# Final blocks in two turns of 128 nodes on one PSUM bank, and a second bank of feature sums for the dense blocks of a graph layer

## The reference

```python
src_h = h[src] @ W_msg.T + b_msg
emb = edge_embed[jnp.clip(edge_type, 0, NUM_EDGE_TYPES)]
messages = jax.ops.segment_sum(src_h + emb, dst, num_segments=num_nodes)
gi = messages @ W_ih.T + b_ih
gh = h @ W_hh.T + b_hh
r = jax.nn.sigmoid(i_r + h_r)
z = jax.nn.sigmoid(i_z + h_z)
n = jnp.tanh(i_n + r * h_n)
h_new = (1.0 - z) * n + z * h
out = layernorm(x + h_new)
```

## Time and profile before

| | before |
|---|---|
| median of 3 runs | 1285.8 us |
| lowest, highest run | 1283.81, 1469.57 us |
| the profiled execution's own time | 1292.56 us |
| its span | 1290.4 us |
| PE busy (matmuls) | 1011.8 us, 78% |
| DVE busy | 846.6 us, 66% |
| ACT busy | 626.9 us, 49% |
| POOL busy | 758.1 us, 59% |
| granted TensorE clock, mean | 0.924 of full speed |

### The profile page before, as it was taken

How to read it: one execution, slowest core, us unless ns; L and a number is a source line. 1 busy time by engine, 2 the same in 40 slices (tenths; PEclk the granted TensorE clock), 3 DMA queues, 4 the chain that set the end, 5 groups by cost and what they waited for, 6 DMA issues and landing times.

```text
span 1290.4 us, 23001 instructions
## 1 busy us (share of the span) xinstructions
PE 1011.8 (78%) x8241; PEld 634.0 (49%) x8241; DVE 846.6 (66%) x2672; ACT 626.9 (49%) x1215; POOL 758.1 (59%) x807
## 2 busy tenths in 40 slices
PE   5535587888888887878888787888888787988794
PEld 1114354555545454555555554555555555555462
DVE  7503557667776676766777667767677677667644
ACT  4342314355545464545655556545565465555523
POOL 7725546565665666566656666656666666566640
PEclk9666588898999999999999999999999999999998
DMA  7629212222323223322323323323333332233331
GB/s 232 177 65 334 74 34 61 75 74 77 78 77 90 73 79 80 90 75 79 90 78 80 87 78 85 82 74 90 79 88 84 84 90 77 79 86 89 84 87 31
DMA packets 95665, 116.97 MB, mean 91 GB/s; under 512 B 20027, under 2 KB 81271, under 8 KB 95544
## 3 DMA queue, kind: packets, MB, share of 16 engines
q0 software_dynamic: 36608, 75.94, 22.1%
...
## 4 chain that ended last, share of the span: by engine, by line
PE 51%; DVE 18%; issue 13%; another core or an unknown queue 9%; ACT 6%; DMA 1%; SPq 1%; DVEq 0%; ACTq 0%
PE psf L1097 20%; PE psb L1082 12%; DVE ohk L862 4%; PE pAB L1026 4%; DVE ohl L868 4%; PE psg L1065 3%; PE pAB L1040 3%; DVE ohk L865 2%; PE psg L1061 2%; ACT mem L1213 2%; PE psg L1069 2%; DVE ohs L844 2%; PE pAB L1043 1%; DMA arena<-in_x 1%
## 5 line engine op out<-in xcount | busy, mean ns | idle before, releaser
L604 POOL DMA_INDIRECT xg<-x_split,idx x676 | 640.8, 948 | 405.4 <-remote 161.1
L1097 PE MATMUL psf<-mem 128*128 128x384 bf16 x2548 | 585.2, 334 | 11.5 <-issue 6.2
L1213 ACT CAST mem<-psb 128x432 f16<-128x432 f32 x832 | 392.9, 524 | 412.0 <-PE psb L1082 286.4
L1082 PE MATMUL psb<-ohk,ohl 128*128 128x108 bf16 (+3 forms) x1801 | 401.1, 263 | 143.4 <-issue 89.5
L862 DVE TENSOR_TENSOR ohk<-table_bank,prm 128x392 bf16<-128x392 f16 (+3 forms) x421 | 260.6, 619 | 113.3 <-PE psb L1082 70.7
L1082 PEld LDWEIGHTS psb<-ohk,ohl 128*128 128x128 bf16 x1801 | 167.7, 100 | 315.8 <-issue 163.7
L1097 PEld LDWEIGHTS psf<-mem 128*128 128x128 f16 x2548 | 223.6, 100 | 108.1 <-issue 30.7
L891 DVE TENSOR_TENSOR mem<-mem,psg 128x120 f32 (+10 forms) x191 | 56.7, 297 | 210.5 <-remote 159.2
L868 DVE TENSOR_TENSOR ohl<-table_bank,prm 128x512 bf16<-128x512 f16 x421 | 174.3, 414 | 0.0
L604 POOL DMA_INDIRECT xg<-in_x,idx x88 | 84.2, 957 | 76.0 <-PE psg L1069 39.7
L865 DVE TENSOR_TENSOR ohk<-table_bank,sort 128x40 bf16<-128x40 f16 (+3 forms) x421 | 102.5, 244 | 0.0
...
## 6 DMA issues: line engine op xcount, KB each, us to landing
...
```

The lines of the kernel that those rows point to most:

```text
L604: pool.indirect_dma_start(out=xg[:, p % RING, :] if split else xg32(p % RING), out_offset=None, in_=x_d if split else x, in_offset=bass.In ...
L1082: ins = pe.matmul(psb[:, bank % NB, held * HC:(held + m) * HC], ohl[:, e % KB, :], ohk[:, e % KB, d * HC:(d + m) * HC], start=(k == 0), st ...
L1097: pe.matmul(psf[:, 0:3 * H], Bb[q % 2][0:kk, HT + h, :], xs[0:kk, h, :, :].rearrange("p c f -> p (c f)"), start=(h == 0), stop=(h == HI - ...
L1213: act.copy(Bb[q % 2][:, :, n:n + MOST], psb[:, bank % NB, 0:MOST * HC].rearrange("p (d h) -> p h d", h=HC)).then_inc(S["s_eb"], 1)
```

## The change

The final blocks but for two get the gates in two turns on one bank: `hh0`, `su0`, `rz0`, `t20` for the first 128 nodes, then `hh1`, `su1`, `rz1`, `t21` for the others. `hh1` waits on PE until `t20` is done (`s_t2` counts halves now). A block then has 13 slots, of which four go with a group (five at the end). The bank that comes free is a second bank of `psf`: the dense blocks use the two in turn, so F pieces wait for the C of the block before last only. S, T and C get the places 0.06, 0.14, 0.19, the F pieces are spread evenly from 0.045 on, and those that pass 1 go over into the next block. DVE's writing of the one-hot matrices of four slots stands behind the slot whose completion it waits for, where that is later than its old place.

```diff
@@ -50,17 +50,18 @@
 FIRST = 4
-STEPS = (3, 4)
+STEPS = (4, 5)
 READY = 10
-SHIFT = 5
+SHIFT = 8
+WIDE_SHIFT = 5
 TURN_AT = (15, 18)
...
 BW = HC * FB // 2
-SETTLED = (0.02, 0.06, 0.10)
-CLEAR = 0.17
+SHIFTED = 0.045
+SETTLED = (0.06, 0.14, 0.19)
 
@@ -164,21 +165,27 @@
 
-STAGES = ("cn", "hh", "su", "rz", "t2", "th", "yt", "bn", "sd", "ln")
-SLOTS = (("cn",), ("hh",), ("su", "rz"), ("t2", "th", "zero"), ("yt",), (), ("bn",), ("sd",), ("ln",))
+STAGES = ("cn", "hh0", "su0", "rz0", "t20", "hh1", "su1", "rz1", "t21", "th", "yt", "bn", "sd", "ln")
+SLOTS = (("cn",), ("hh0",), ("su0", "rz0"), ("t20",), ("hh1",), ("su1", "rz1"), ("t21", "th", "zero"), ("yt",), (), ("bn",),
+         ("sd",), ("ln",))
+WIDE = ("hh", "su", "rz", "t2")
+WIDE_SLOTS = (("cn",), ("hh",), ("su", "rz"), ("t2", "th", "zero"), ("yt",), (), ("bn",), ("sd",), ("ln",))
+
+
+SECOND = (NBLK - 3, NBLK - 1)
 
...
 def dense_units():
-    units, late = [], []
+    units, late, rest = [], [], []
     for q in range(NQ + 1):
...
         pe = sum(0.03 + 0.045 * DS[u[1]][1] for u in own) + 0.35 * len(parts)
-        free = CLEAR if late else 0.0
-        mixed = sorted([((k + 0.5) / len(own), u) for k, u in enumerate(own)] +
-                       [(free + (1 - free) * (k + 0.5) / PARTS, u) for k, u in enumerate(parts)] +
-                       [(at, u) for at, (_, u) in zip(SETTLED, late)])
+        timed = [(SHIFTED + (k + 0.5) / PARTS, u) for k, u in enumerate(parts)]
+        mixed = sorted([((k + 0.5) / len(own), u) for k, u in enumerate(own)] + rest +
+                       [t for t in timed if t[0] < 1] + [(at, u) for at, (_, u) in zip(SETTLED, late)])
+        rest = [(at - 1, u) for at, u in timed if at >= 1]
         span = max(dve / 0.67, pe / 0.70)
@@ -187,7 +194,15 @@
             late = [(0.0, (kind, q - 1)) for kind in "STC"]
-    return units + late
+    return units + [(0.0, u) for _, u in rest] + late
+
+
+def slots_of(i):
+    return WIDE_SLOTS if i in SECOND else SLOTS
+
+
+def shift_of(i):
+    return WIDE_SHIFT if i in SECOND else SHIFT
 
@@ -218,15 +233,15 @@
         else:
-            free = len(active) < 2 and (not active or done >= SECOND[0] or len(SLOTS) - len(active[-1]) >= SHIFT - 1)
+            free = len(active) < 2 and (not active or done >= SECOND[0] or len(slots_of(done - 1)) - len(active[-1]) >= shift_of(done - 1) - 1)
         b = pick(g, top) if free and done < NBLK - 1 else None
...
             slots = [[(s, done, b) for s in slot if s != "zero" or b >= CB0]
-                     for slot in SLOTS]
+                     for slot in slots_of(done)]
             if b >= CB0:
...
                 if b + 1 < NBLK and (BN * (b + 1) - ND) % R == 0:
-                    slots[5].append(("wrap", b + 1))
+                    slots[slots_of(done).index(())].append(("wrap", b + 1))
             done += 1
@@ -433,11 +450,11 @@
         psb = pb("psb", [P, NB, 512])
-        psf = pb("psf", [P, 512])
+        psf = pb("psf", [P, 2, 512])
         table_bank = pb("table_bank", [P, 512])
         psg = pb("psg", [P, 512])
-        pAB = pb("pAB", [P, 2, 512])
-        xbank = [pAB[:, 0, :], pAB[:, 1, :], psf[:, :]]
+        pAB = pb("pAB", [P, 1, 512])
+        xbank = [pAB[:, 0, :], psf[:, 0, :], psf[:, 1, :]]
         numbers_words = table_bank[:, 0:MOST * HC // 2]
@@ -792,11 +812,13 @@
                 st, mv, sd, rs = stats(i, slow)
-                if kind == "t2":
-                    v.wait_ge(S["s_rz"], i + 1)
-                    v.wait_ge(S["s_pm"], i + 1)
-                    link(v.tensor_tensor(tn[:, 0, :, :], pAB[:, :, 3 * H:4 * H], rz[:, :, 0:H], ALU.mult))
-                    v.tensor_tensor(tn[:, 1, :, :], tn[:, 0, :, :], pAB[:, :, 0:H], ALU.add).then_inc(S["s_t2"], 1)
+                if kind[:2] == "t2":
+                    _, h, n = part_of(kind)
+                    v.wait_ge(S["s_rz"], 2 * i + h + n)
+                    v.wait_ge(S["s_pm"], 2 * i + h + n)
+                    link(v.tensor_tensor(tn[:, 0, h:h + n, :], pAB[:, :, 3 * H:4 * H], rz[:, h:h + n, 0:H], ALU.mult))
+                    v.tensor_tensor(tn[:, 1, h:h + n, :], tn[:, 0, h:h + n, :], pAB[:, :, 0:H], ALU.add
+                                    ).then_inc(S["s_t2"], n)
                 elif kind == "yt":
@@ -900,13 +922,13 @@
                             v.wait_ge(S["s_tt"], q)
-                        v.tensor_reduce(added[:, :], psf[:, 0:3 * H].rearrange("p (c f) -> p f c", c=3), AX, ALU.add
+                        v.tensor_reduce(added[:, :], psf[:, q % 2, 0:3 * H].rearrange("p (c f) -> p f c", c=3), AX, ALU.add
                                         ).then_inc(S["s_sc"], 1)
...
                         weights()
-                    elif it[0] in STAGES or it[0] == "zero":
+                    elif it[0] in STAGES + WIDE or it[0] == "zero":
                         final(*it, False, BEFORE[(it[0], it[1])] if it[0] == "cn" else seen)
@@ -916,7 +938,9 @@
                         else:
-                            ahead.setdefault(own[a - back] if a >= back else ("G", 0), []).append(it)
+                            e = it[1] - KB + min(OB, SLOTS_N - it[1]) - 1
+                            at = ("B", max(own[a - back][1], min(t for t in TOLD if t >= e))) if a >= back else ("G", 0)
+                            ahead.setdefault(at, []).append(it)
                 for it in ahead[None]:
@@ -1009,24 +1033,30 @@
                 pe.matmul(pAB[:, 0, 0:3 * H], wms[:, :], wih[:, :], start=True, stop=True, skip_group_check=True)
-                pe.matmul(pAB[0:ND2, 1, 0:3 * H], embs[:, :], wih[:, :], start=True, stop=True,
+                pe.matmul(psf[0:ND2, 1, 0:3 * H], embs[:, :], wih[:, :], start=True, stop=True,
                           skip_group_check=True).then_inc(S["s_wp"], 1)
...
             def final(kind, i, b, slow, seen):
+                if kind[:2] not in WIDE:
+                    return
                 pAB = buffers(i, slow)[0]
-                if kind == "hh":
-                    if second(i, slow) and not gone(i, slow):
+                parts, h, n = part_of(kind)
+                if kind[:2] == "hh":
+                    if h:
+                        pe.wait_ge(S["s_t2"], 2 * i + 1)
+                    elif second(i, slow) and not gone(i, slow):
                         pe.wait_ge(S["s_eb"], BANKS)
                     elif i:
-                        pe.wait_ge(S["s_t2"], gone(i, slow))
+                        pe.wait_ge(S["s_t2"], 2 * gone(i, slow))
                     else:
...
                     pe.wait_ge(s_x[i % 2], 16 * (i // 2 + 1))
-                    for s in range(2):
-                        ins = pe.matmul(pAB[:, s, H:4 * H], xb[:, i % 2, s * P:(s + 1) * P], whh[:, :], start=True, stop=False,
+                    for s in parts:
+                        ins = pe.matmul(pAB[:, s - h, H:4 * H], xb[:, i % 2, s * P:(s + 1) * P], whh[:, :], start=True, stop=False,
                                         skip_group_check=True)
-                    ins.then_inc(S["s_hh"], 1)
-                elif kind == "su":
+                    if h + n == 2:
+                        ins.then_inc(S["s_hh"], 1)
+                elif kind[:2] == "su":
                     if slow:
@@ -1036,13 +1066,13 @@
                     sums = den if b < CB0 else whole[:, 0, b * BN:(b + 1) * BN] if slow else ring[:, 0, ring_at(b)]
-                    for s in range(2):
-                        pe.matmul(pAB[:, s, 0:3 * H], sums[:, s * P:(s + 1) * P], wihc[:, :], start=False, stop=False,
+                    for s in parts:
+                        pe.matmul(pAB[:, s - h, 0:3 * H], sums[:, s * P:(s + 1) * P], wihc[:, :], start=False, stop=False,
                                   skip_group_check=True)
-                    for s in range(2):
-                        ins = pe.matmul(pAB[:, s, :], cnts[:, table_of(i, slow), s * P:(s + 1) * P], emw[:, :],
+                    for s in parts:
+                        ins = pe.matmul(pAB[:, s - h, :], cnts[:, table_of(i, slow), s * P:(s + 1) * P], emw[:, :],
                                         start=False, stop=True, skip_group_check=True)
-                    ins.then_inc(S["s_pm"], 1)
+                    ins.then_inc(S["s_pm"], n)
 
@@ -1090,29 +1120,31 @@
                                 pe.wait_ge(S["s_xl"], UNITS)
+                            elif q == 1:
+                                pe.wait_ge(S["s_wc"], 1)
                             else:
-                                pe.wait_ge(S["s_cp"], q)
+                                pe.wait_ge(S["s_cp"], q - 1)
                         for h in range(HI * f // PARTS, HI * (f + 1) // PARTS):
                             kk = P if h < HI - 1 else TAIL
-                            pe.matmul(psf[:, 0:3 * H], Bb[q % 2][0:kk, HT + h, :],
+                            pe.matmul(psf[:, q % 2, 0:3 * H], Bb[q % 2][0:kk, HT + h, :],
                                       xs[0:kk, h, :, :].rearrange("p c f -> p (c f)"),
...
```

(25 more changed lines are left out.)

18 lines of the change are left out of this document (11 added, 7 removed).

## The result

| | before | after |
|---|---|---|
| median | 1285.6 us (4 runs) | 1354.3 us (4 runs) |
| lowest, highest | 1283.81, 1469.57 us | 1345.78, 1356.91 us |
| span of the profiled execution | 1290.4 us | 1344.0 us |
| PE busy | 1011.8 us | 1035.4 us |
| PE idle (span less busy) | 278.6 us | 308.6 us |

The changed kernel is slower: ratio 1.052, 95% interval [1.044, 1.060]. I had forecast 1305 us and 1272 to 1338; the time is outside. One of the four runs of the kernel before, the one of 1469.57 us, was in a slow state and doesn't count in the ratio. One thing has to be known for all that follows: in the experiments the kernel before took 1044 to 1046 us in the median on each of five chips, and not 1286, and the same change cost there 1.067 [1.062, 1.071]. No run here shows what makes the difference between 1286 and 1044; it is taken up at the end.

A forecast was written before the change was run, and what follows sets the result against it. The prediction took POOL's gather loop as the bound. Its terms, 23 - 6 + 2 = +19 us, took the profiled 1292.56 us to 1311.6; with the runs' median 6.8 us lower it forecast 1305 us, range 1272 to 1338.

The forecast's parts named there:

- The price of the new wait: Final blocks, hh1 on PE waiting for t20: each stretch late by 0.5 us, 46 x 0.5 = 23 us, ends 0 and 64.
- 4.65 us of work: PE's work left from going on at hh1 to the end of the next group, over 6.2 us behind the signals.
- The bound: Middle stage, 600 to 1200 us: POOL's gather loop sets the time, 6.14 us a group; most of PE's idle time is slack.
- The slots: Final blocks: thirteen slots at four a group are 3.25 groups a block, where nine at three were 3.
- Split work: Final blocks, two more instructions on DVE and one on ACT per block: costs nothing; matmuls the same in number and shape.
- The dense blocks: Second bank of sums removes PE's waits at T and F: -6 us, with 0 and 20 us gained as ends.
- VectorE's writing: DVE's matrices for B behind the slot they wait for: moves waits on DVE, counted inside the 20 us.
- the 20 us: All that any PE work can give back in POOL's waits, 200 to 1226 us: 163 x 0.12 = 20 us.
- Rival 3: The wait at hh1 costs its upper price through ACT's late sigmoid: 1.4 us a block, 1346 us, slower; chance 0.30.
- Rival 2: PE is the bound, its waits at T, F and DVE's matrices come back: about -50, 1236 us, faster; chance 0.09.
- Rival 1: The wait at hh1 fits into PE's slack, only small terms are left: around 1282 us, within 2%; chance 0.20.

The follow-up runs named there:

- e6: The changed kernel as it is, on the chip of the experiments: 1114.4 us, 1.067 against the kernel before.
- e7: The changed kernel with hh1 one slot later, together with su1 and rz1: 1071.9 us, 1.027 against the kernel before.
- e9: The kernel before with every second gather of 128 rows left out from tile 120 on: 1044.1 us, 1.001 against the kernel before.
- e13: The changed kernel with hh1 moved earlier, into the slot of t20: 1145.8 us, 1.097 against the kernel before.
- e5: The kernel before, unchanged, on the chip of the experiments: 1044.35 us in one run, median of seven more 1044.3.
- e12: The changed kernel with one bank of feature sums, the old dense places, and hh1 one slot later: 1066.7 us, 1.021 against the kernel before.
- e8: The changed kernel with VectorE writing the dense tiles' matrices at the kernel before's places: 1132.3 us, 1.085 against the kernel before.

## Why the prediction was wrong

*The price of the new wait.* This is the step of the sum that failed: the term "46 x 0.5 = 23 us". The place, the count and the length of the wait were right. I said 40 to 46 times and 1 to 3 us; it is 43 times, 95.6 us, 2.2 us each. PE goes on 1.26 to 1.58 us behind the start of GA in all 45 cycles; I had 1.55 behind the signals. But a cycle with `t20` got 1.3 us longer, and not 0.5: 7.85 us for 6.56, 55 us in 43 cycles. The term rested on 4.65 us of work from there to the end of the next group. In e6, at a granted clock of 0.99 in the mean, that stretch has a median of 4.88 us, and in the profile of the result it takes 4.90 us in the 22 cycles where the clock stayed up, so the work was sized rightly to 0.25 us. In the 23 others it takes 6.66 us. I had priced PE's stop as a shift in time, and left out that what comes behind it may run at the lower level. 23 cycles with 1.76 us more are 40 us, most of the 49 between my 1305 and the measured 1354. That is an estimate from the trace, and no run tested it; why the clock falls behind some stops and not behind others is open. At 1044 us the clock plays no part, the stops are 0.9 us each, and the change still costs 70 us, of which 42.5 go with the stop, by e7.

*The bound.* I read POOL's row that fills the window as proof that the gather loop is the bound and that PE has slack. It proves nothing, as e9's row shows. What the row did say is that 141 of its 230.8 us of idle time were waits for PE. The even bursts are a better sign, and they are real: in the profile before, 141 of the 161 bursts between 240 and 1320 us start within 6.25 us of the one ahead, and in the profile after 115 of 161; the lost time sits in the cycles with `t20`. That fits the loop that I had described, and doesn't prove it. At 1044 us there are no such bursts. There e9 leaves half of the gathers out and the time stays, and e7 and e13 move PE's stop and the time follows in full, so PE has no slack. Whether it had some at 1286 us, where signals were seen 1.2 us after a burst and PE was 78% busy, stays open, since no experiment ran in that condition.

*The slots.* `SLOTS` of the changed kernel has twelve entries, not thirteen, so that a block takes three groups at the least, as before, and not 3.25. With four steps in a group the stages keep their places in it, and `t20` meets GA in 46 of 47 blocks. The sum didn't use the 3.25.

*Split work.* "Nothing, as long as DVE's idle time is there" left out PE. Two matmuls of one kind in a row are now one: the mean of the counts' product went from 542 ns (L1043 in e5; 550 in rows 7) to 702 ns (L1073 in e6). The ends of matmuls are modelled, so this is the profile's account. PE's busy time grew by 10.5 us in e12, where it hardly stops, and PE waits 7 to 10 us more for the count table in e6 and e12.

*The dense blocks.* I took -6, between -20 and 0. F's wait for C is gone in the profile of the result (4.2 us before), and T's waits went from 24.1 + 6.4 us to 4.5 + 5.4, the second number each time what the profile calls "issue". But the new places cost more than that gives: +5 to +13 us in three pairs at 1044 us. There the sign was wrong; at 1286 us the dense part wasn't run alone.

*VectorE's writing* I had put inside the 20 us. At 1044 us it keeps 18 us off the price of the turns (e8).

*The rivals.* Rival 3 gave 1346 us and its sign, POOL's waits growing by 0.3 us or more in the mean (0.43), came out. Its mechanism didn't: in none of the 45 cycles is `t20` held up beyond what I had, and the added delay comes after PE has gone on. Rival 2, PE as the bound, was right about the engine in the experiments, and wrong about the sign, since I set the waits that go against only "some stalls" at hh1. Rival 1 is refuted.
